# Gated recurrence, six layers on one core: other pairs turned by DMA in layer 0, wider unbounded gathers, a later second total

## The reference

```python
def _L0_rec_ref(state, token, ih, hh):
    n_layers = ih.shape[0]                      # 6
    for i in range(n_layers):
        gate = ih[i][token]                     # ih: 6 x 4000 x 256
        state = jnp.tanh(state + jnp.matmul(state, hh[i]) * gate)
    return state                                # 2048 x 256 fp32
```

## Time and profile before

| what | value |
|---|---|
| median of 3 runs | 102.38 us (102.11 to 102.92) |
| profiled execution, its own time | 102.9 us |
| its span, first to last instruction | 101.1 us |
| mean granted TensorE clock | 0.954 of full |
| DMA packets, bytes | 27368, 14.25 MB |

### The profile page before, as it was taken

How to read it: one execution, slowest core, us unless ns; L and a number is a source line. 1 busy time by engine, 2 the same in 40 slices (tenths; PEclk the granted TensorE clock), 3 DMA queues, 4 the chain that set the end, 5 groups by cost and what they waited for, 6 DMA issues and landing times.

```text
span 101.1 us, 1829 instructions
## 1 busy us (share of the span) xinstructions
PE 86.9 (86%) x664; PEld 76.0 (75%) x664; DVE 80.1 (79%) x128; ACT 77.5 (77%) x133; POOL 68.2 (67%) x63
## 2 busy tenths in 40 slices
PE   5209999969995299999999999999999999999910
PEld 5108588948883277999999999999999999988800
DVE  1159966697660775789999899998999999989990
ACT  5059999799871266789699998999989978992641
POOL 3578787777772045477698868987499949879000
PEclk9999999999999655999999999999999999999995
DMA  1899899953999405057255551544545425964984
GB/s 23 286 338 392 258 280 314 334 186 96 70 107 169 53 3 110 0 104 59 52 104 102 104 104 35 112 82 90 104 60 121 81 55 104 96 118 82 367 310 174
DMA packets 27368, 14.25 MB, mean 141 GB/s; under 512 B 23772, under 2 KB 24028, under 8 KB 27360
## 3 DMA queue, kind: packets, MB, share of 16 engines
q1 hardware_dynamic: 24864, 12.07, 52.1%
q0 software_dynamic: 2496, 2.07, 10.1%
HBM read 17.31 MB, written 2.10 MB: 192 GB/s over the span
## 4 chain that ended last, share of the span: by engine, by line
PE 55%; DVE 17%; DMA 13%; issue 7%; POOL 6%; ACT 0%; SPq 0%; DVEq 0%; POOLq 0%
PE products L296 46%; DMA gates<-in_gate_rows,index 8%; PE turned L328 8%; DVE gates L430 6%; POOL gates L273 6%; DMA last_rows<-in_gate_last 5%; DVE sums L468 4%; DVE sums L480 4%; DVE split_cols L485 1%; DVE sums L465 1%; DVE split_rows L492 1%; PE spare L345 1%; ACT state L403 0%; SPq L225 0%; POOLq L273 0%
## 5 line engine op out<-in xcount | busy, mean ns | idle before, releaser
L296 PE MATMUL products<-w_head,split_cols 128*128 128x256 f16 x316 | 57.1, 279 | 0.0
L280 POOL TENSOR_TENSOR sums<-sums,state 128x512 f32<-128x512 f32 x36 | 45.6, 1272 | 16.9 <-DVE sums L468 16.5
L296 PE MATMUL products<-w_rest,split_cols 128*128 128x256 f16 x158 | 44.1, 279 | 0.0
L403 ACT ACTIVATE state<-sums 128x512 f32<-128x512 f32 (+1 forms) x49 | 30.4, 619 | 15.2 <-DVE sums L480 7.3
L296 PEld LDWEIGHTS products<-w_head,split_cols 128*128 128x128 f16 x316 | 31.9, 101 | 4.0
L468 DVE SCALAR_TENSOR_TENSOR sums<-products,w_down,gates 128x512 f32<-128x512 f32 (+1 forms) x40 | 29.5, 738 | 4.8 <-PE products L296 4.8
L288 PE MATMUL products<-w_full,first_cols 128*128 128x256 f32 x64 | 18.0, 430 | 4.6 <-DMA w_full<-in_weights 4.4
L288 PEld LDWEIGHTS products<-w_full,first_cols 128*128 128x128 f32 x64 | 13.3, 218 | 7.4 <-issue 4.7
L296 PEld LDWEIGHTS products<-w_rest,split_cols 128*128 128x128 f16 x158 | 15.8, 100 | 2.1
L273 POOL DMA_INDIRECT gates<-in_gate_rows,index x12 | 13.2, 1097 | 3.7 <-issue 3.4
L367 ACT ACTIVATE gates<-last_rows 128x1536 f32<-128x1536 f32 (+1 forms) x8 | 10.6, 1390 | 4.1 <-DMA last_rows<-in_gate_last 4.1
(11 more groups left out here) (37 smaller groups left out, 40.0 us busy)
## 6 DMA issues: line engine op xcount, KB each, us to landing
first_cols<-in_state_cols SPq DMA_DIRECT2D x8, 256.0 KB, 4.1
out<-state SPq DMA_DIRECT2D x7, 256.0 KB, 2.4
w_full<-in_weights SPq DMA_DIRECT2D x6, 256.0 KB, 5.4
last_rows<-in_gate_last SPq DMA_DIRECT2D x1, 768.0 KB, 4.9
split_cols<-split_rows SPq DMA_TRANSPOSE x20, 3.0
state<-in_state_rows SPq DMA_DIRECT2D x1, 256.0 KB, 6.2
out<-state SPq DMA_DIRECT2D x2, 128.0 KB, 1.7
gates<-in_gate_rows,index POOLq DMA_INDIRECT x12, 4.8
```

What stands on the lines that cost most here:

```text
L280: nc.gpsimd.tensor_tensor(sums[:, q], sums[:, q], pair_rows(state, q), ALU.add).then_inc(pool_added, 1)
L296: last = nc.tensor.matmul(bank[:, j, :], split_cols[:, q, s, j, k, :], w[:, l - 1, k * HID:(k + 1) * HID], start=(n == 0), stop=(n == len( ...
L403: nc.scalar.activation(pair_rows(state, q)[:, cut], sums[:, q, cut], ACT.Tanh).then_inc(state_ready, 1)
```

## The change

Three kinds of numbers change. In layer 0 pairs 2, 5 and 6 are turned by DMA and pairs 0, 1, 3, 4, 7 by TensorE (before: 1, 3, 5, 7 and 0, 2, 4, 6); the later layers stay. The four unbounded gathers bring two layers' gates, and the bounded ones of those tiles four. Pair 7's old state comes by a load instead of a TensorE turn, the fills go to other engines and steps, and the totals, scales, first and second parts, weight sums and weight loads stand at other steps.

```diff
--- before.py
+++ after.py
@@ -34,7 +34,8 @@
 
 
     DMA_PAIRS = (1, 3, 5, 7)
-    PE_INSTEAD = ()
+    PE_INSTEAD = ((0, 1), (0, 3), (0, 7))
+    DMA_INSTEAD = ((0, 2), (0, 6))
 
     TURN_LAG = 3
     HEAD_LAG, HEAD_ROWS_LAG = 3, 1
@@ -47,17 +48,18 @@
 
 
     FIRST = (0, 1, 2, 3)
+    FIRST_LAYERS = 2
     GATHERS = (4, 5, 6, 7, 8, 9, 10, 11, 12, 13, 14, 15, 0, 1, 2, 3)
-    ACT_FILLS = {-1: (5, 7, 10, 12, 14, 0, 1), 1: (2,)}
-    DVE_FILLS = {-1: (4, 6, 8, 9, 11, 13), 0: (15,), 2: (3,)}
+    ACT_FILLS = {-1: (4, 6, 8, 10, 12, 14, 1), 0: (15, 2)}
+    DVE_FILLS = {-1: (5, 7, 9, 11, 13, 3), 0: (0,)}
 
 
     GROUPS = ((0, 1), (1, SPLIT))
-    SUMS_AT = {0: 0, 2: 1, 3: 2, 4: 3, 5: 4}
-    TOTALS_AT = {3: 0, 8: 1}
-    SCALES_AT = {2: 0, 7: 1}
-    HEADS_AT = {1: 0, 7: 1, 9: 2, 21: 3, 29: 4}
-    RESTS_AT = {2: 0, 13: 1, 21: 2, 29: 3, 35: 4}
+    SUMS_AT = {0: 0, 1: 1, 2: 2, 4: 3, 5: 4}
+    TOTALS_AT = {3: 0, 9: 1}
+    SCALES_AT = {3: 0, 11: 1}
+    HEADS_AT = {2: 0, 10: 1, 13: 2, 25: 3, 32: 4}
+    RESTS_AT = {4: 0, 12: 1, 19: 2, 27: 3, 36: 4}
 
     WARM = 4
     TOP = 14
@@ -65,16 +67,17 @@
     MANTISSA, BIAS = 23, 127
     INDEX_STEPS, SCALE_STEPS = 3, 4
 
-    LOAD_LAG = 6
+    LOAD_LAG = 5
 
     AHEAD = 2
-    WEIGHTS_WITH = {0: (0, 1, 2), 3: (3,), 4: (4,), 5: (5,)}
-
-    ROWS_BY_PE = (1, 2, 3, 4, 5, 6, 7)
+    WEIGHTS_WITH = {0: (0, 1, 2), 2: (3,), 6: (4,), 7: (5,)}
+
+    ROWS_BY_PE = (1, 2, 3, 4, 5, 6)
     PRODUCTS, TURNED, COPIES = 3, 2, 2
 
     def by_dma(i):
-        return order[i][0] < LAST and order[i][1] in DMA_PAIRS and order[i] not in PE_INSTEAD
+        layer, q = order[i]
+        return layer < LAST and (q in DMA_PAIRS and (layer, q) not in PE_INSTEAD or (layer, q) in DMA_INSTEAD)
 
     def by_pe(i):
         return order[i][0] < LAST and not by_dma(i)
@@ -260,14 +263,15 @@
                 return bass.IndirectOffsetOnAxis(ap=index[:, t:t + 1], axis=0)
 
             for t in FIRST:
-                pool.indirect_dma_start(gates[:, t, 0, :], None, gate_first, offset(t)).then_inc(first_in[t // PAIR], 16)
+                pool.indirect_dma_start(gates[:, t, :FIRST_LAYERS, :].rearrange("p l h -> p (l h)"), None, gate_first,
+                                        offset(t)).then_inc(first_in[t // PAIR], 16)
             for t in GATHERS:
                 if t in by_act:
                     pool.wait_ge(act_filled, by_act.index(t) + 1)
                 else:
                     pool.wait_ge(vector_filled, by_vector.index(t) + 1)
                 if t in FIRST:
-                    pool.indirect_dma_start(gates[:, t, 1:, :].rearrange("p l h -> p (l h)"), None, gate_later, offset(t),
+                    pool.indirect_dma_start(gates[:, t, FIRST_LAYERS:, :].rearrange("p l h -> p (l h)"), None, gate_later, offset(t),
                                             bounds_check=VOCAB - 1, oob_is_err=False).then_inc(gates_in[t // PAIR], 16)
                 else:
                     pool.indirect_dma_start(gates[:, t].rearrange("p l h -> p (l h)"), None, gate_rows, offset(t),
@@ -363,7 +367,7 @@
         def _(act):
             def fill(t):
                 act.wait_ge(last_in, 16)
-                lo = 1 if t in FIRST else 0
+                lo = FIRST_LAYERS if t in FIRST else 0
                 nc.scalar.activation(gates[:, t, lo:, :].rearrange("p l h -> p (l h)"), last_rows[:, lo * HID:],
                                      ACT.Copy).then_inc(act_filled, 1)
 
@@ -457,7 +461,7 @@
                 dve.wait_ge(product_ready, i + 1 + n)
                 if layer == 0:
                     dve.wait_ge(first_in[q] if PAIR * q in FIRST else gates_in[q], 16 * PAIR)
-                elif layer == 1 and PAIR * q in FIRST:
+                elif layer == FIRST_LAYERS and PAIR * q in FIRST:
                     dve.wait_ge(gates_in[q], 16 * PAIR)
                 product = product_bank(i, cut)[:, cut]
                 g = pair_rows(gates, q)[:, cut, layer, :]
@@ -541,7 +545,7 @@
     tiles, chunks = rows // 128, hid // 128
 
     gate_rows = ih.transpose(1, 0, 2).reshape(vocab, layers * hid)
-    gate_first = _np.concatenate([gate_rows[:, :hid], _np.repeat(gate_rows[-1:, :hid], 127, axis=0)])
+    gate_first = _np.concatenate([gate_rows[:, :2 * hid], _np.repeat(gate_rows[-1:, :2 * hid], 127, axis=0)])
     host = {
         "token": token,
         "state_cols": state.reshape(128, tiles // 2, 2, chunks, 128).transpose(1, 4, 3, 2, 0).reshape(
@@ -549,7 +553,7 @@
         "state_rows": state.reshape(128, tiles, hid),
         "weights": hh.reshape(layers, chunks, 128, hid).transpose(0, 2, 1, 3),
         "gate_first": gate_first,
-        "gate_later": gate_rows[:, hid:],
+        "gate_later": gate_rows[:, 2 * hid:],
         "gate_rows": gate_rows,
         "gate_last": _np.repeat(gate_rows[-1:], 128, axis=0),
     }
```

## The result

The changed kernel is slower: 109.59 us, median of 6 runs (108.18 to 110.78), against 102.98 for the kernel before (102.11 to 103.91, 6 runs). The ratio is 1.056, 95% interval 1.049 to 1.064. The forecast was 96.5. The profiled execution took 110.43 us with a span of 108.6 and a mean clock of 0.926.

A forecast was written before the change was run, and what follows sets the result against it. TensorE was taken to bound the steady part, so gains lay before 42.5 us: 42.58 - 36.46 - 0.2 = 5.9 us saved, 102.9 to 97.0, less 0.5 to the median: 96.5 us, range 95.4 to 99.6.

The forecast's parts named there:

- walk of TensorE's stream: TensorE's pieces timed with the old kernel's pitches: product 5 at 22.49 us (before 22.85), second total done at 32.26.
- The part that was to bring the gain: From product 8's start to the end of step 8's turn: 12.36 us before, 7.22 forecast, 5.1 of the 5.9 saved.
- one late gather costs twice: Before 42.5 us, tile 15's late gather costs about 3.0 us of TensorE standing and another 3 us of half speed.
- a rule about transposes and gathers: At 25.0 to 27.5 us: 256 KB transposes and gathers hurt each other far more than their bytes say.
- Steady part: From 42.5 to 90 us: bound by TensorE, 3.06 us per two steps, left alone by the change.
- First total, 0.34: Two fills now precede the first weight sum, ending at 18.86 us, so TensorE waits 0.34 us at the first total.
- Wider gathers, 0.7: At the start: 0.52 MB more ahead of pair 1's columns delays TensorE by 0.7 us, bounds 0 and 1.3.
- rival C: Issuing unbounded gathers costs by width, 4 x 1.18 us more on POOL, tile 15 landing at 37.3: 105.6 us; chance 0.06.
- Tile 15's gather and the second total: With the transpose later, the gather lands at 30.0 us, is added at 31.3, and the second total's wait is gone.
- Pair 2's transpose: Needed by product 10: issued at 26.8 us, takes 5.6, lands at 32.4, before TensorE's 32.96.
- rival B: The wait moves to product 10: transpose takes 8.9 us, TensorE waits 2.7, the clock falls: 102.7 us, no change; chance 0.16.
- Late scales, 0.2 us: Group 1's scales behind step 11 in layer 1: VectorE lags up to 2 us, 0.2 added for a waiting turn.

The follow-up runs named there:

- b0: The kernel before, unedited, run again on chip 6: 98.18 us, ratio 0.999 to the kernel before.
- a0: The changed kernel, unedited, on chip 6: 99.93 us, ratio 1.016 to the kernel before.
- a1: The changed kernel, unedited, on chip 14: 98.74 us, ratio 1.006 to the kernel before.
- e1: The changed kernel with the four unbounded gathers bringing one layer again, on chip 11: 110.14 us, ratio 1.037 to the kernel before.
- e2: The kernel before with only the unbounded gathers widened to two layers, on chip 11: 106.45 us, ratio 1.002 to the kernel before.
- s1: The changed kernel with second total, its scales and first part of layer 2's weights at their old steps, chip 14: 98.47 us, ratio 1.004 to the kernel before.
- a2: The changed kernel, unedited, on chip 13, where the kernel before takes 105.72 us: 109.01 us.
- u1: The changed kernel with one-layer first gathers and the 16 bounded gathers replaced by unbounded ones, true lookups left out, on chip 1: 110.08 us.
- u2: The changed kernel with the last eight bounded gathers left out, VectorE waiting for those tiles' fills instead, on chip 1: 100.14 us.
- f2: The kernel before with only the changed kernel's fills, on chip 13: 106.21 us, ratio 1.017 to the kernel before.
- f1: The kernel before with only the changed kernel's fills, on chip 6: 98.21 us, ratio 1.010 to the kernel before.
- s2: The kernel before with only second total, its scales and first part of layer 2's weights moved later, chip 14: 98.42 us, ratio 0.995 to the kernel before.
- d1: The changed kernel with the 16 bounded gathers' bound set to row 0, so they carry hardly any bytes, chip 14: 97.50 us, ratio 0.997 to the kernel before.

## Why the prediction was wrong

**The step that failed**, as the compared pair shows it, is in the walk of TensorE's stream: "Product 5 starts at 22.49 where it started at 22.85, although a turn and a wait are new ahead of it: VectorE no longer has a fill, four scale pieces and a second part ahead of step 3, so TensorE no longer waits there for its add." That wait was put at nothing, and it was 8.02 us; product 5 started at 33.51. The walk let a reader go on as soon as TensorE's piece was done, and in after TensorE's updates came 4 to 9 us behind their pieces. No rival of mine had that. The part that was to bring the gain did bring it in this pair: 5.8 us between steps 8 and 13.

A second step failed as a price of the kernel, though not as a reading of its trace: "So one late gather costs twice: about 3.0 us of standing and, until the clock is back, another 3 us of half speed." The kernel before has neither the wait nor the dip on group Q (b0), and there the change brought nothing: a0 is 0.6 us behind b0 at step 8 and 1.8 at steps 14 and 46. The trace of before held a hint that I passed by. Its transfers were slow at one place (84 GB/s at a DMA share of 1.41), and I took that for a rule about transposes and gathers, on one execution. The Trainium skill (Advanced Engine Details and Errata, X-Bar Transpose (TRN2)) has the rule that I set aside, that transposing DMAs are as fast as regular ones. It stands better, with 4.3 us in b0 beside gathers; the 8.9 us of before stays unexplained. Nor does a gather need a transpose beside it to be slow: tile 11's in a1, issued at 19.5 us, took 6.0 and cost VectorE a wait of 1.48, before the first transposing DMA was issued.

Point by point:

- *Steady part:* right. Steps 14 to 46 take 48.03 us in both.
- *First total, 0.34:* unimportant, as forecast; the first total stands between products 3 and 4 with no idle time of its own in after.
- *Wider gathers, 0.7:* right in kind. Pair 1's product starts 1.9 us later in the compared pair, but one pair says little, since it starts at 12.77 in a0 and 11.90 in a1, the same kernel. Over all traces it starts at 12.0 on average with one layer (ten kernels, 11.25 to 12.69) and at 12.7 with two (ten, 11.90 to 13.37). e1 and e2 find nothing of it in the time. POOL's issue cost nothing for the width (0.96 to 1.45 us each, before 0.96 to 1.44), so rival C's mechanism is out, though its sign came true.
- *TensorE's stream:* product 5 was to start at 22.49 and started at 33.51; in a0, without late releases, at 25.60. In a0 products 4 and 5 are 2.61 us apart, as walked (1.73 and two of 0.44). So the pitches were right, and the assumption that a finished piece is at once seen by its reader was not.
- *Tile 15's gather and the second total:* nothing waits for either in after, as forecast, but everything around them came some 13 us later than in the walk, which makes it a weak test. In a0 nothing waits for them either.
- *Pair 2's transpose (rival B):* no wait at product 10; the transpose issued at 39.1 in after took 3.4 us, the one of a0 4.1.
- *Late scales, 0.2 us:* the place was right, the size was 0.9, because the four pieces of scales took VectorE 1.87 us beside GpSimd's adds (39.41 to 41.28 in a0) and 0.55 without them (s1).

**What the runs show, and what they leave open.** Shown: in the compared pair the loss is TensorE's updates being seen late; such updates appear on group L while gathers are issued (a2, u1), and with eight gathers less they end sooner and the time falls (u2). Not shown: why the changed kernel loses more than the kernel before, since variants of both have late releases on group L (a2; f2 and e2). Its gathers are issued as those of before are, one per 1.3 us, and end at the same time (the last is issued at 29.5 and 29.9). My guess is that more handovers between TensorE and VectorE fall in the stretch, which I haven't counted. Of the parts, the fills cost 1 to 1.7% in the kernel before (f1, f2), and the sum isn't explained. The trace of before in the comparison has no late release; its three later runs, next to those of after, took 103.05 to 103.91 us and left no trace. So part of the 1.056 may be the condition that the chip was in, a rival that nothing here rules out. Open too: what in the gathers does it (their issue on GpSimd, their descriptors, their landings; u2 takes away all three), and what sets the groups of chips apart. Last, all timed runs here were recorded as well, and records are missing just in the stretch where updates are late. The Trainium skill (NOTIFIC — Programmer's Manual, "When the ring fills") says that a queue of records that is full can drop new ones, overwrite old ones or stall the engine that makes them. Whether the recording takes part in the waits, no run here shows.

## What to carry to other kernels

Before you price a wait, look at a second execution of the same kernel, best on another chip: here a wait of 3.3 us, on which a whole change was built, wasn't in the next one, and the same kernel took 98.4 to 106.9 us by chip. Where a view names no releaser for an idle time of several microseconds, compare it with the time at which the work waited for was done and with the record of its update, and count the records of updates by stretch. Look at where small VectorE pieces on the critical path fall beside GpSimd's adds: here 0.17 us became 1.19 beside them (a0), and stayed 0.17 between two of them (s2).

## What the runs showed of the hardware

- Five of TensorE's semaphore updates were recorded 4 to 9 us after their work was done while a row of indirect DMAs was under way (after), and waits of the same kind stand in the traces of chips 11, 13 and 1 (6.4 us in e1, 5.76 in a2, 9.33 in u1). The records of updates fell from 20 to 30 a microsecond to 3 to 5, for the last part with little moved (0 to 69 GB/s from 27 to 38 us in after).
- The first transposing DMA took 8.9 us in one execution (before) and 4.3 in another of the same kernel (b0); tile 15's gather took 7.93 and 4.5.
- A VectorE operation on 128x4 integers took 172 ns alone (s1) and 1190 beside GpSimd's `tensor_tensor` of 128x512 (a0).
- A gather with nothing to bring is still issued in the same time (0.99 us for most in d1 as in after), and leaving out the looked-up rows gained 1.2 us in the median (d1 97.50, a1 98.74), which the intervals don't settle.
